# Turning a head's row maxima behind the second pair of score products instead of behind the first, in a decoder layer's cross-attention

## What is computed

```python
def _L0_xattn_ref(q, k, v):
    b, d, m = q.shape
    c = v.shape[1]
    h = 8
    qh = q.reshape(b * h, d // h, m)
    kh = k.reshape(b * h, d // h, -1)
    vh = v.reshape(b * h, c // h, -1)
    scale = 1.0 / jnp.sqrt(jnp.asarray(d // h, dtype=q.dtype))
    qk = jnp.einsum('bdm,bdn->bmn', qh, kh) * scale
    sm = jax.nn.softmax(qk, axis=-1)
    ret = jnp.einsum('bmn,bcn->bcm', sm, vh)
    return ret.reshape(b, c, m)

x = x + _L0_attn_ref(_layernorm(x), Wq, Wk, Wv, Wo)
x = x + _L0_xattn_ref(_layernorm(x), ctx, ctx)
x = x + _L0_ffn_ref(_layernorm(x), w_gate, w_up, w_down)
```

## Time and profile before

| | us |
|---|---|
| median of three runs | 846.62 |
| lowest and highest of them | 846.23, 850.64 |
| the profiled execution, its own time | 845.78 |
| its span, first to last instruction | 844.0 |

### The profile page before, as it was taken

How to read it: one execution, slowest core, us unless ns; L and a number is a source line. 1 busy time by engine, 2 the same in 40 slices (tenths; PEclk the granted TensorE clock), 3 DMA queues, 4 the chain that set the end, 5 groups by cost and what they waited for, 6 DMA issues and landing times.

```text
span 844.0 us, 14277 instructions
## 1 busy us (share of the span) xinstructions
PE 770.0 (91%) x4258; PEld 410.0 (49%) x4306; DVE 662.2 (78%) x1939; ACT 469.4 (56%) x828; POOL 411.9 (49%) x418
## 2 busy tenths in 40 slices
PE   5899889999999999998886799999997998999996
PEld 3677634444444444445664455444443343444442
DVE  6667668898898988962777877888885888899983
ACT  3465456676776767773222566666664554344451
POOL 3354469999994000001222377777777444433321
PEclk9999979999999999998999699999998999999998
DMA  8598745435531121201557455555552124444553
GB/s 303 175 333 305 238 161 167 149 105 169 149 118 54 57 64 49 72 3 53 167 194 245 134 153 174 163 161 162 162 152 58 28 61 95 100 88 88 89 94 94
DMA packets 112317, 113.62 MB, mean 135 GB/s; under 512 B 70640, under 2 KB 82544, under 8 KB 109168
## 3 DMA queue, kind: packets, MB, share of 16 engines
q1 hardware_dynamic: 105392, 91.66, 38.7%
q0 software_dynamic: 1728, 12.58, 4.3%
q10 hardware_dynamic: 5120, 8.46, 2.8%
HBM read 81.26 MB, written 20.51 MB: 121 GB/s over the span
## 4 chain that ended last, share of the span: by engine, by line
PE 21%; DVE 13%; issue 6%; POOL 5%; SPq 4%; DMA 3%; ACT 2%; DVEq 0%; ACTq 0%; POOLq 0%
PE r_p L1415 5%; PE r_pn L1372 3%; DVE r_mx L1195 2%; PE r_pn L1431 2%; DMA r_rden<-inverse_sums 2%; PE r_p L1335 2%; PE r_p L1360 2%; PE r_p L1361 2%; POOL r_h L1042 2%; DVE r_stats L1161 2%; DVE r_h L1234 2%; PE r_pd L1431 2%; PE r_pd L1382 1%; DVE r_lo L1169 1%; DVE tok L1175 1%
## 5 line engine op out<-in xcount | busy, mean ns | idle before, releaser
L147 DVE CUSTOM_DVE_ANT_0 b_junk<-b_p,mask_qk 128x128 bf16<-128x128 f32 x480 | 204.4, 484 | 34.3 <-PE b_p L127 33.9
L702 ACT ACTIVATE b_probs<-b_p 128x512 f32<-128x512 f32 (+1 forms) x352 | 176.9, 560 | 32.7 <-PE b_p L764 13.2
L127 PE MATMUL b_p<-ks,qs 96*128 96x128 bf16 x480 | 116.9, 304 | 13.6 <-PEq L197 6.6
L764 PE MATMUL b_p<-qs,ks 98*128 98x512 bf16 (+1 forms) x352 | 123.1, 364 | 2.2 <-DMA qs<-mrow 1.1
L1085 ACT ACTIVATE r_probs<-r_p 128x512 f32<-128x512 f32 x128 | 74.3, 593 | 65.1 <-PE r_p L1361 63.9
L1195 DVE TENSOR_REDUCE r_mx<-r_p 128x1 f32<-128x512 f32 x128 | 84.8, 684 | 14.4 <-PE r_p L1335 13.3
L1016 POOL TENSOR_TENSOR r_halves<-r_probs 128x1024 f32<-128x1024 f32 x32 | 76.5, 2390 | 24.4 <-ACT r_probs L1085 22.3
L127 PEld LDWEIGHTS b_p<-ks,qs 96*128 96x128 bf16 x480 | 42.5, 99 | 69.7 <-issue 14.1
L779 PE MATMUL b_pv<-b_probs,v 128*32 128x512 f32 (+3 forms) x1024 | 75.6, 436 | 0.0
L1135 ACT ACTIVATE r_silu<-r_p,r_cg 128x512 f32<-128x512 f32 x64 | 42.3, 680 | 52.9 <-PE r_p L1415 51.0
L1415 PE MATMUL r_p<-wu,r_zt 128*128 128x512 bf16 x251 | 65.1, 379 | 4.4 <-DVE r_h L1234 4.1
(11 more groups left out here) (156 smaller groups left out, 1620.1 us busy)
## 6 DMA issues: line engine op xcount, KB each, us to landing
r_k<-in_ctx SPq DMA_DIRECT2D x64, 128.0 KB, 2.7
r_qh<-x_normed_high SPq DMA_DIRECT2D x64, 128.0 KB, 2.7
q_parts<-a_parts SPq DMA_DIRECT2D x16, 384.0 KB, 6.8
qs<-q_parts SPq DMA_DIRECT2D x32, 192.0 KB, 3.2
a_wst<-in_w_gate SPq DMA_DIRECT2D x4, 1024.0 KB, 9.2
a_wst<-in_w_up SPq DMA_DIRECT2D x4, 1024.0 KB, 11.3
a_wst<-in_w_down SPq DMA_DIRECT2D x4, 1024.0 KB, 9.8
qs<-q_parts SPq DMA_DIRECT2D x32, 128.0 KB, 2.7
```

The source lines that it names most:

```text
L127: last = nc.tensor.matmul(st.bank(keep, i, k)[:, c:c + w], keep["qs"][0:STACK, s, j, qt * P:(qt + 1) * P], keep["ks"][0:STACK, s, 0:w], st ...
L147: best = nc.vector.tensor_tensor_reduce(out=junk[:, 2 * (st.use[i, k] % slots) + n, 0:w], in0=bank[:, c:c + w], in1=keep["mask_qk"][:, SEQ ...
L702: nc.scalar.activation(pblock(j % 2, kb)[:, j0:j0 + nj, c:c + w], p2[(NE * j + n) % BANKS2][:, 0:nj * w].rearrange("p (j c) -> p j c", j=n ...
L764: last = nc.tensor.matmul(bank, ks[0:STACK + 2, s, kb * P:(kb + 1) * P], qs[0:STACK + 2, s, j0:j0 + nj, kb * P + c:kb * P + c + w], start= ...
```

## The change

The turn is moved one place later. On TensorE it stands behind F(1) S(1) instead of behind F(0) S(0). On VectorE `mrow` stands behind `maximum(1)` instead of before it. The numbering of bank uses follows. All else, the order on SyncE, ScalarE and GpSimd among it, is as before, and the number of instructions is the same.

```diff
-        TURN = 1
+        TURN = 2
 
         def use(i, k):
 
             if i == 1:
-                return max(k - 1, 0)
+                return k if k < TURN else k - 1
             return 4 + 5 * (i - 2) + k if i <= HEADS_X else 4 + 5 * (HEADS_X - 1)
...
                 def maximum(n):
                     if 1 <= i <= HEADS_X:
-                        k = n if n == 0 else n + 1
+                        k = n if n < TURN else n + 1
...
                 maximum(0)
+                maximum(1)
                 j = i - 2
                 if 0 <= j < HEADS_X:
                     dve.wait_ge(p1_full, use(i, TURN) + 1)
...
                     nc.vector.tensor_scalar(mrow[:, j % UNROLL, :], p1[use(i, TURN) % BANKS][0:KD, 0:P], -1.0, None, ALU.mult).then_inc(p1_used, 1)
-                maximum(1)
...
-                    j, k = i - 1, n if n == 0 else n + 1
+                    j, k = i - 1, n if n < TURN else n + 1
...
                 for n in range(KD):
                     first_scores(n)
                     second_scores(n)
-                    if n == 0:
+                    if n == TURN - 1:
                         turn_maxima()
```

## The result

The changed kernel takes 851.96 us in the median of 20 runs, the kernel before 846.42 in as many. The ratio is 1.0048, with a 95% interval of 1.003 to 1.0066: slower by about 4.1 us (2.5 to 5.6). The two medians differ by more than that, 5.5 us, but within this interval. The profiled execution of the changed kernel took 850.57 us with a span of 848.8 (before: 845.78 and 844.0). Busy times are the same within 0.3%: PE 767.9 us, DVE 663.0, ACT 469.4, POOL 412.7.

A forecast was written before the change was run, and what follows sets the result against it. A loop of GpSimd and VectorE, 11.28 us per two steps, was taken as the bound. Losses of 0.6 + 0.6 + 0.76 + 1.83 = 3.8 us gave 849.6 us profiled, 850.4 us median, range 847.0 to 852.6.

The forecast's parts named there:

- What bounds the kernel: Cross-attention from step 11: a loop of GpSimd and VectorE sets the beat, 11.28 us for two steps.
- What the turn's move takes away: TensorE's wait at the turn: moving it gains 0, since the wait lies in slack.
- The row 2.71 us behind y: Loop through SyncE and rden, common case: 2.71 + 6.10 + 2.35 = 11.16 us, 0.12 under the beat, no loss.
- Steps 13 to 31: Ten intervals between multiplications y: three with long SyncE issues lose 0.61 us each, 1.83 in all.
- The start: Up to the first y in step 11: losses of 0.6, 0.6 and 0.76 us, sum 1.96.
- The tail: Behind step 31: the last maxima row costs 0 and the feed-forward part is only shifted.
- Rival one: Steps 13 to 31: rden's loop takes over in every interval, 852.6 us or half the extra, 851.5; chance 0.36.
- Rival two: Steps 3 to 11: the start's loss is absorbed in slack, giving 849.2 or 848.4 us; chance 0.17.
- Rival three: TensorE's wait at the turn was worth something: up to 4.0 us faster, 842.6 us; chance 0.05.

The follow-up runs named there:

- TURN = 0: The kernel before, with the turn in front of the first pair of scores and mrow in front of maximum(0); ratio 1.0022 to the kernel before.
- row-late half: The kernel before, with mrow behind maximum(1) on VectorE but TensorE's turn left behind the first pair; ratio 1.007 to the kernel before.
- TURN = 3: The turn behind the third pair of scores and mrow behind maximum(2); 898.22 us, ratio 1.0591 to the kernel before.
- the moved addition: The kernel before, with GpSimd adding y to the tokens between its two additions of the next step; alone, ratio 1.0067 to the kernel before.

## Why the prediction came out as it did

The forecast was 850.4 us against 846.62, a ratio of 1.0045; measured is 1.0048. The total is right within its noise, two of its terms are not, and part of the agreement is luck. In the two traces the cross-attention lost 5.2 us, not 3.8: the forecast had the start 0.9 too large and the intervals 2.3 too small. The last y stands at 634.24, just where the prediction put it (634.2), only because the entry was by chance 1.40 us earlier as well.

*What bounds the kernel.* Right. In the changed kernel kk ends 10.53 to 10.57 us behind y in all ten intervals, as before, and the six undisturbed intervals are 11.28 to 11.32. Halving GpSimd's addition shortened them.

*What the turn's move takes away: 0.* Right. The wait went to F(2), 0.23 us in each even step of the loop, and with `TURN = 0` even 3.9 us of additional waiting on TensorE had no effect on the ten intervals.

*The row 2.71 us behind y, 6.10 on SyncE, 2.35 to land, and 0.12 of slack left.* Right, row by row: 2.70; 6.09 to 6.11; and 2.33 to 2.57 in the four intervals in which y waited, 2.24 to 2.34 in the undisturbed ones with the halved addition. The row-late half alone carried the loss, and rden issued early took back that of the intervals.

*Steps 13 to 31, 1.83 us.* Right in mechanism, too small: 4.15 measured. There are four long intervals, not three, and they cost 1.18, 0.59, 0.97 and 1.36 us over what they were, not 0.61 each. The step that failed is "three of the ten intervals have such a long issue", with 6.94 us as its length. In the changed kernel the long ones are 7.36 to 7.38 us three times and 6.81 once. Their number and length were read from one trace. The second trace of the kernel before has 6.69, 6.73 and 6.43 instead of three times 6.94 to 6.98. The length varies from trace to trace, but the places don't vary freely. Take the nine traces with rden last in its step and `TURN` 0 to 2. In all nine the second interval (SyncE's step 15) and the seventh (step 25) have a long issue, 6.66 to 7.56 and 6.30 to 7.48 us; the fourth (step 19) has one in six and the tenth (step 31) in five. The other six intervals have 6.09 to 6.13 in every trace. The tenth made the difference in number here: SyncE's long issue fell in step 30 before, ahead of the row that counts, and in step 31 after. On SP:

```profile
620.15 1.41 SPq L948 DMA_DIRECT2D inverse_sums<-r_inv  x1
```

```profile
628.07 2.10 SPq L954 DMA_DIRECT2D r_vt<-in_ctx_t  x2
```

The first is the kernel before, where 0.58 us is usual, the second the changed one, where 1.14 is. Before, 0.7 us of slack took in all but the last 0.1 to 0.2 us of each; the change left 0.1 to 0.2 of slack, and nearly all of each counted.

*The start, 1.96 us.* Too large in this trace, 1.04. S(0) of step 3 gave 0.25, not 0.6: the row had landed in 1.96 us (468.74 to 470.70), so at the 2.30 of the earlier trace rows S(0) had not been waiting for it, and the "2.30 later" was no landing time. S(0) of step 6 stood 0.56 late, not 1.2. The first y came another 0.48 later, not 0.76. In the other traces with a late row at `TURN` 1 or 2 the start varies: 59.81, 59.05, 59.49, 58.27 and 57.54 us, against 56.31 to 56.93 in six with the row where it was. So 1.96 was a fair middle, and the two errors cancel in part here. That a later row lengthens the start stands on this separation; by which waits, beyond S(0) of steps 3 and 6, wasn't tried, and `TURN = 0` has a start of 57.90 with an early row.

*The tail, 0.* Right: 17.30 against 17.27 us to S(0) of step 34.

*Rival one*, every interval: no, six of ten are unchanged, and the half addition showed the loop 0.14 to 0.24 below the beat. Its word for the long intervals, that they would cost more, was the true part. *Rival two*, an absorbed start: no. *Rival three*, the wait was worth something: no, none of the kernels with the late turn was faster than its counterpart with the early one.

## What to carry to other kernels

A wait that the table shows is worth moving only if it lies in the loop that sets the beat; here 2.9 of TensorE's 4 us lay in the ten intervals, in slack, and 3.9 us more of it there left their sum within 0.2 us. What is moved later takes its whole queue with it: compare the loop through that queue with the beat, and don't stop at a positive margin. A margin smaller than the occasional delays of issue and landing (here up to 1.3 us, in four of ten rounds) is a loss, of about the excess times its frequency. These delays are to be read from several traces, round by round: some come back at the same place of the program, with another length, and one trace shows one length and hides what the slack takes in.

## What the runs showed of the hardware that I had not expected

Two transfers issued in a row by SyncE take 1.10 to 1.17 us as a rule (1.33 for the context rows of many even steps), but in each of the 14 traces some take 1.6 to 2.6. They are 24 to 35 us apart in the two kernels compared, and come back, in most of the traces, in steps 15, 19, 25 and 30 or 31, though not always at the same instruction. With `TURN = 3` two steps last 14.7 us instead of 11.3, and the long issues still stand in steps 15, 19, 25 and 31 (1.77, 1.54, 1.61 and 1.67 us), now 33 to 44 us apart. So they go with the place in the program rather than with time. Why wasn't tried, and stays open.

A transfer's landing is 2.0 to 2.6 us as a rule and was 3.0 to 4.0 in single cases. And kk or y, VectorE instructions with two SBUF inputs, when they meet a running addition of GpSimd, end 0.53 to 0.57 us behind it in all of these traces, whatever is left of that addition. The prediction had this from kk; that y is caught as well, and took 2.86 us for 0.69 of work, came with the moved addition.
